# A mixture-of-experts layer behind linear attention: the router with its weights stationary, 32x32 transposes on VectorE, and residual sums with the second statistics ahead of the routing

## The reference

```python
Q, K, V = x @ wq.T, x @ wk.T, x @ wv.T                 # 64 wide
energy  = einsum('bnd,bne->bde', K, V)                 # over the 2048 tokens
out     = (Q @ energy * sqrt(3 / 64)) @ wo.T
```

```python
scores = sigmoid(x @ Wr)                               # 8 experts
idx    = top_k(scores + router_bias, 2)
w      = scores[idx] / (sum(scores[idx]) + 1e-9)       # cw: w at idx, 0 elsewhere
hid    = silu(x @ Wg[e]) * (x @ Wu[e])                 # e = 0..3, 128 wide
routed = sum_e cw[e] * (hid[e] @ Wd[e]) + (cw[4] + cw[6]) * x + cw[7] * relu(x)
out    = routed + causal_depthwise_conv(x, 4 taps) + conv_b
```

## Time and profile before

| | us |
|---|---|
| median of 3 timed runs (892.45 to 894.4) | 893.69 |
| the profiled execution | 893.6 |
| its span, from the first instruction to the last | 891.8 |

### The profile page before, as it was taken

One profiled execution on the slowest core, in us unless ns is written; L12 is line 12 of the kernel. 1 busy time (PEld: TensorE's weight loads), 2 busy tenths in 40 slices (PEclk: granted clock), 3 DMA queues, 4 the chain that ended last, 5 costly groups with the idle time before them and its releaser, 6 DMA issues.

```text
span 891.8 us, 16729 instructions
## 1 busy us (share of the span) xinstructions
PE 855.9 (96%) x5437; PEld 754.3 (85%) x5437; DVE 741.1 (83%) x2056; ACT 628.7 (71%) x1238; POOL 572.7 (64%) x654
## 2 busy tenths in 40 slices
PE   5789999999999999999999999999999999999997
PEld 4668989898888888988889888888888898788876
DVE  5758889988888998888898888899888887767775
ACT  5676777777687777778677777777777775655643
POOL 3336776667676657667666767666576766556663
PEclk9989999999999999999999999999999999999999
DMA  9111434543334543343544343454424344433333
GB/s 286 57 52 47 137 121 142 143 117 99 95 119 142 144 142 68 114 129 120 143 143 114 101 115 99 143 144 142 119 72 119 101 114 119 111 104 100 106 91 84
DMA packets 79446, 103.86 MB, mean 116 GB/s; under 512 B 6528, under 2 KB 58880, under 8 KB 79360
## 3 DMA queue, kind: packets, MB, share of 16 engines
q1 hardware_dynamic: 74752, 86.02, 30.4%
q0 software_dynamic: 4608, 16.78, 10.0%
HBM read 68.96 MB, written 17.04 MB: 96 GB/s over the span
## 4 chain that ended last, share of the span: by engine, by line
PE 66%; DVE 13%; POOL 12%; issue 5%; ACT 4%; DMA 0%; POOLq 0%; ACTq 0%; DVEq 0%
PE ps_gu L406 9%; PE ps_gu L408 9%; PE ps_gu L407 9%; POOL enx L1368 7%; PE ps_y L406 5%; PE ps_y L408 5%; PE ps_y L407 5%; PE ps_sh L543 4%; PE ps_sh L533 3%; POOL gate L1327 3%; PE ps_sh L516 2%; DVE stats L1065 2%; DVE acc L1057 2%; ACT x L840 2%; PE ps_y L456 2%
## 5 line engine op out<-in xcount | busy, mean ns | idle before, releaser
L1327 POOL TENSOR_TENSOR gate<-gate,cwb 128x512 f32<-128x512 f32 x128 | 167.5, 1309 | 127.8 <-ACT gate L763 126.4
L406 PE MATMUL ps_gu<-x2T_hi,wgu_hi 128*128 128x512 f32 x512 | 212.2, 414 | 0.0
L408 PE MATMUL ps_gu<-x2T_hi,wgu_lo 128*128 128x512 f32 x512 | 203.0, 396 | 0.0
L407 PE MATMUL ps_gu<-x2T_lo,wgu_hi 128*128 128x512 f32 x512 | 202.2, 395 | 0.0
L1368 POOL TENSOR_TENSOR enx<-inv_e,logits 128x32 f32<-128x32 f32 x32 | 177.5, 5546 | 8.6 <-ACT logits L756 8.6
L406 PE MATMUL ps_y<-wd_hi,hid_hi 128*128 128x256 f32 x512 | 152.8, 299 | 4.0 <-DVE hid_lo L1018 3.1
L1029 DVE SCALAR_TENSOR_TENSOR conv<-x2T,conv_w,conv 128x512 f32<-128x512 f32 x192 | 146.4, 801 | 0.0
L408 PE MATMUL ps_y<-wd_hi,hid_lo 128*128 128x256 f32 x512 | 145.3, 284 | 0.0
L407 PE MATMUL ps_y<-wd_lo,hid_hi 128*128 128x256 f32 x512 | 144.2, 282 | 0.0
L1011 DVE TENSOR_TENSOR hid<-ps_gu,gate 128x512 f32<-128x512 f32 x128 | 86.0, 672 | 39.2 <-POOL gate L1327 38.1
L408 PEld LDWEIGHTS ps_gu<-x2T_hi,wgu_lo 128*128 128x128 f32 x512 | 96.9, 189 | 22.5
(11 more groups left out here) (115 smaller groups left out, 1934.3 us busy)
## 6 DMA issues: line engine op xcount, KB each, us to landing
cwb<-cw_rows SPq DMA_DIRECT2D x128, 256.0 KB, 4.0
xa<-in_x SPq DMA_DIRECT2D x32, 512.0 KB, 7.5
acc<-in_x SPq DMA_DIRECT2D x32, 512.0 KB, 6.7
acc<-x POOLq DMA_DIRECT2D x32, 512.0 KB, 4.6
out<-acc SPq DMA_DIRECT2D x64, 256.0 KB, 2.3
cwb<-in_wg SPq DMA_DIRECT2D x4, 128.0 KB, 4.0
cwb<-in_wu SPq DMA_DIRECT2D x4, 128.0 KB, 3.8
cwb<-in_wd SPq DMA_DIRECT2D x1, 512.0 KB, 4.5
```

Source lines behind the costliest of these rows:

```text
L406: nc.tensor.matmul(dst, a_hi, b_hi, start=start, stop=False, skip_group_check=True)
L407: nc.tensor.matmul(dst, a_hi, b_lo, start=False, stop=False, skip_group_check=True)
L408: return nc.tensor.matmul(dst, a_lo, b_hi, start=False, stop=stop, skip_group_check=True)
L1327: g.tensor_tensor(gate[:, e % 2], gate[:, e % 2], cwb[:, q, e], ALU.mult).then_inc(gatew_ready, 1)
```

## The change

- **Router.** The stationary operand is now `wr2`: per half of the features 32 columns, of which 8 are the rounded `wr`, 8 its rest and 16 zero. Two matmuls run the rounded x2T past it and two the rest of x2T, each with 512 columns (all four tiles). The result is the transposed logits, 32 rows by 512.
- **Logits.** `logits_turn` on VectorE transposes them in 32x32 blocks out of PSUM and adds the high and the low half (`summed`, on 32 partitions). Four DMAs on SP (`move_logits`) lay them out on 128 partitions. ScalarE computes `size = |logits|`, `mag = size + 2**-100` and `dip = silu(-mag)`; VectorE makes the sigmoid of it, `minor = dip / mag`, `signed = (logits > 0) + minor`, `score = |signed|`. The power and `den` on GpSimd go.
- **Weights.** The 1e-9 is a ninth column of `raw`, so `wsum_eps` goes. A VectorE transpose in 32x32 blocks makes `cwT`, four DMAs store it. TensorE's `weights_transpose` and ScalarE's copy go.
- **Order.** `residual` and `norm2_stats` stand ahead of the routing in every step, which is in two halves (`route_scores`, `route_weights`); in `drain` steps `hid_low(2)` stands between them. `norm1_stats` moves behind `hidden(1)`, tap 1 ahead of the first `x2T_low`, tap 2 is split around the outputs. `halo` moves from VectorE to ScalarE. In `drain` steps `hid_high(2)` stands ahead of `silu(3)` and both ahead of `conv_begin`.
- **Head.** The first five transposes of xn use other banks and stand between Q, attention and Gram matrices in another order; attention of group 1 comes behind the first router; the first SiLU is asked for at once.

The core of the diff (the heads of ScalarE, VectorE and GpSimd are reordered to match):

```diff
+        wr2 = sb("wr2", [P, HC, SQ], F32R)
...
+            def move_logits(st):
+
+                sp.wait_ge(sum_ready, st.before("R", 1, 1))
+                if st.later("R", 1):
+                    sp.wait_ge(cw_ready, st.before("R"))
+                for j in range(P // SQ):
+                    sp.dma_start(logits[j * SQ:(j + 1) * SQ, :], summed[:, j].rearrange("p t e -> p (t e)"))\
+                        .then_inc(logits_loaded, 16)
+
             def spread_weights(st):
 
                 k = st.slot("R", 2)
                 rows = cw_rows[bass.ds(st.group("R"), 1)]
                 sp.wait_ge(cwT_ready, st.before("R", 1, 1))
-                sp.dma_start(rows.rearrange("a e (t n) -> (a e t) n", t=TG), cwT[:, :]).then_inc(cw_stored, 16)
-                sp.wait_ge(cw_stored, st.before("R", 16, 16))
+                for j in range(P // SQ):
+                    sp.dma_start(rows[:, :, :].rearrange("a e (t n) -> (a e t) n", t=TG)[:, j * SQ:(j + 1) * SQ],
+                                 cwT[j * SQ:j * SQ + EM * TG, :]).then_inc(cw_stored, 16)
+                sp.wait_ge(cw_stored, st.before("R", 64, 64))
...
+                    move_logits(st)
                     spread_weights(st)
...
             def router(st):
-                pe.wait_ge(x2T_ready, st.before("R", HC, HC))
+                if st.before("R") == 0:
+                    pe.wait_ge(wrlo_out, 1)
+                b, q = ps_sh[0][0:SQ, :], st.slot("R", 2)
                 pe.wait_ge(x2Tlo_ready, st.before("R", HC, 1))
-                b, q = ps_sh[0], st.slot("R", 2)
-                for t in range(TG):
-                    for c in range(HC):
-                        last = nc.tensor.matmul(b[:, t * NE:(t + 1) * NE],
-                                                x2T[:, q, c, PAD + t * P:PAD + (t + 1) * P], wr_sb[:, c],
-                                                start=(c == 0), stop=(c == HC - 1))
+                pe.wait_ge(x2Thi_ready, st.before("R", HC, HC))
+                for c in range(HC):
+                    nc.tensor.matmul(b, wr2[:, c], x2T_hi[:, q, c], start=(c == 0), stop=False,
+                                     skip_group_check=True)
+                for c in range(HC):
+                    if c == 1:
+                        pe.wait_ge(x2Tlo_ready, st.before("R", HC, HC))
+                    last = nc.tensor.matmul(b, wr2[:, c], x2T_lo[:, q, c], start=False, stop=(c == HC - 1),
+                                            skip_group_check=True)
                 last.then_inc(router_done, 1)
...
-                if st.before("B") == 0:
-                    pe.wait_ge(xnTlo_ready, 2 * HC - h)
-                elif st.before("B") == 1:
-                    pe.wait_ge(x1_ready, 1 + h)
-                elif h == 0:
+                if st.before("B") == 1:
+                    pe.wait_ge((x2Tlo_ready, turn_ready)[h], (HC, 1)[h])
+                elif st.before("B") > 1 and h == 0:
                     pe.wait_ge(x2Tlo_ready, st.before("R", HC, HC))
-                else:
-                    pe.wait_ge(logits_ready, st.before("R", 1, 1))
+                elif st.before("B") > 1:
+                    pe.wait_ge(turn_ready, st.before("R", 1, 1))
...
-            def weights_transpose(st):
-                pe.wait_ge(cw_ready, st.before("R", 1, 1))
-
-                if st.before("R") == 0:
-                    pe.wait_ge(xnTlo_ready, 5 * HC)
-                elif st.on("B"):
-                    pe.wait_ge(x1_ready, st.before("B", 2, 1))
-                else:
-                    pe.wait_ge(x2Tlo_ready, st.before("R", HC, HC))
-                nc.tensor.transpose(ps_sh[1][0:EM * TG, 0:P],
-                                    cw[:, st.slot("R", 2), 0:EM].rearrange("p e t -> p (e t)"), ident[:, :])\
-                    .then_inc(cwT_done, 1)
...
+                head_transpose(0)
                 pe.wait_ge(w_loaded, 16 * N_LOADS)
                 chain_gramT(b)
                 chain_p1(b)
                 chain_et(b)
+                q_project(at("Q", 0, NG))
                 pe.wait_ge(et_out, b.chains(2, 2))
                 chain_f(b)
+                attention(b, 0)
+                attention(b, 1)
+                head_transpose(1)
+                gram_matrix(at("A", 4, NG))
+                head_transpose(2)
                 q_project(at("Q", 1, NG))
-                for n in range(2):
-                    attention(at("B", n, NG), 0)
-                    attention(at("B", n, NG), 1)
-                gram_matrix(at("A", 4, NG))
-                r = at("R", 0, NG)
                 x2_transpose(r, 0)
                 x2_transpose(r, 1)
+                gram_matrix(at("A", 5, NG))
                 router(r)
-                xn_transpose(at("A", 2, NG), 0)
-                xn_transpose(at("A", 2, NG), 1)
-                xn_transpose(at("A", 3, NG), 0)
-                xn_transpose(at("A", 3, NG), 1)
+                attention(at("B", 1, NG), 0)
+                attention(at("B", 1, NG), 1)
...
-                if r_on:
-                    weights_transpose(st)
+                if b_on and drain:
+                    down(st, "C", 2)
                 if a_on and r_on:
                     xn_transpose(st, 0)
-                if c_on:
+                if c_on and not (b_on and drain):
...
-            def logits_copy(st):
-                act.wait_ge(router_done, st.before("R", 1, 1))
-
+            def halo(st):
+
+                q = st.slot("R", 2)
                 if st.later("R", 1):
-                    act.wait_ge(enx_ready, st.before("R"))
-                copy(logits[:, :], ps_sh[0][:, 0:TG * NE]).then_inc(logits_ready, 1)
+                    act.wait_ge(x2T_ready, st.before("R", HC))
+                if st.later("R", 2):
+                    act.wait_ge(conv_ready, st.before("R", CT, -CT))
+                if st.first("R"):
+                    copy(x2T[:, q, :, 0:PAD], ident[:, 0:HC * PAD].rearrange("p (c n) -> p c n", c=HC), 0.0)\
+                        .then_inc(halo_ready, 1)
+                else:
+                    copy(x2T[:, q, :, 0:PAD], x2T[:, 1 - q, :, GT:GT + PAD]).then_inc(halo_ready, 1)
+
+            def score_size(st):
+                act.wait_ge(logits_loaded, st.before("R", 64, 64))
+                if st.later("R", 1):
+                    act.wait_ge(cw_ready, st.before("R"))
+                nc.scalar.activation(size[:, :], logits[:, :], ACT.Abs).then_inc(size_ready, 1)
+                act.wait_ge(size_ready, st.before("R", 1, 1))
+                nc.scalar.activation(mag[:, :], size[:, :], ACT.Identity, bias=least[:, :]).then_inc(mag_ready, 1)
+
+            def score_dip(st):
+
+                act.wait_ge(mag_ready, st.before("R", 1, 1))
+                nc.scalar.activation(dip[:, :], mag[:, :], ACT.Silu, scale=-1.0).then_inc(dip_ready, 1)
...
+                if r_on:
+                    score_size(st)
+                    score_dip(st)
+                if c_on:
                     q = st.slot("C", 2)
                     act.wait_ge(skip_ready, st.before("C", 2, 2))
                     for t in range(TG):
@@ -966,15 +997,16 @@
                     for t in range(TG):
                         nc.scalar.activation(x2[:, q, t], x2[:, q, t], ACT.Relu, scale=cw[:, q, EM + 3, t:t + 1])\
                             .then_inc(relu_ready, 1)
+                if c_on and st.drain():
+                    hid_high(st, 2)
+                    silu(st, 3)
...
+                dve.wait_ge(mag_ready, st.before("R", 1, 1))
+                done(v.reciprocal(rmag[:, :], mag[:, :]))
+                dve.wait_ge(dip_ready, st.before("R", 1, 1))
+                after()
+                done(v.tensor_tensor(minor[:, :], dip[:, :], rmag[:, :], ALU.mult))
+                after()
+                done(v.scalar_tensor_tensor(signed[:, :], logits[:, :], 0.0, minor[:, :], ALU.is_gt, ALU.add))
+                after()
+                done(v.scalar_tensor_tensor(flat(score[:, :, :]), signed[:, :], -1.0, signed[:, :], ALU.mult, ALU.max))
...
+                dve.wait_ge(cw_ready, st.before("R", 1, 1))
+                if st.later("R", 1):
+                    dve.wait_ge(cw_stored, st.before("R", 64))
+                v.transpose(cwT[:, :], cw[:, q].rearrange("p e t -> p (e t)")).then_inc(cwT_ready, 1)
+
+            def logits_turn(st):
+                dve.wait_ge(router_done, st.before("R", 1, 1))
+                v.transpose(turned[:, :, :, :].rearrange("p j t n -> p t j n"),
+                            ps_sh[0][0:SQ, :].rearrange("p (t j n) -> p t j n", t=TG, j=P // SQ))\
+                    .then_inc(turn_ready, 1)
+                dve.wait_ge(turn_ready, st.before("R", 1, 1))
+                if st.later("R", 1):
+                    dve.wait_ge(logits_loaded, st.before("R", 64))
+                v.tensor_tensor(summed[:, :, :, :].rearrange("p j t e -> p (j t) e"),
+                                turned[:, :, :, 0:NE].rearrange("p j t e -> p (j t) e"),
```

(71 more changed lines are left out.)

261 lines of the change are left out of this document (133 added, 128 removed).

## The result

The changed kernel takes 932.14 us (median, 929.65 to 936.26) where the kernel before took 894.05 in the same session. The ratio is 1.041, with a 95% interval of 1.038 to 1.045: slower, where I had predicted 880 and faster. The profiled execution has a span of 931.0 us, before 891.8: 39.2 us to explain.

A forecast was written before the change was run, and what follows sets the result against it. TensorE was taken to set the pace, VectorE not far behind; after the change VectorE would make plain steps later. 893.6 + 8.6 (plain) - 6 (chain) - 5 (start) - 11 (end) = 880.2 us; range 854 to 901.

The forecast's parts named there:

- TensorE's part: Router and weights transpose on TensorE: 0.88 us less per step, a plain step 24.5 if nothing else bound it.
- VectorE's sum: VectorE's work from first x2T_lo to hid_lo(2): 17.6 us, making hid_lo(2) ready at 23.0 and a plain step 24.9.
- the collision with tap 2: Plain steps: tap 2's half waits 1.1 us on VectorE for GpSimd's second gate product; plain step 25.8.
- +8.6 us: The 19 plain steps together: 0.45 us more each than now.
- There is about 0.6 us of slack, which I cost at nothing: ScalarE waits for the logits DMAs until 14.7; 9 us of work behind fit before norm1's followers are wanted at 23.
- the second collision: Rival: small routing operations meet the fourth gate product, 1.1 us a step, 901 us; chance 0.18, shared with slow transpose.
- -6: Seven chain steps: TensorE has 3 us more work, hid_lo(2) is in time, so 0.88 us saved in each.
- -11: Last four steps, 768 to 866 us: no wait for cw, shorter router, 21.7 us each, 11 us gained.
- -5: Start: first pass of the loop 2 us earlier, its router 3 us cheaper; between 0 and -9.
- The reorder: VectorE: residual and norm2_stats ahead of the routing add 3.11 us before hid_lo(2); raw, no longer held, gives back 0.88.

The follow-up runs named there:

- late_turn: The version at 887 us with the turn and sum of the logits moved on VectorE from ahead of tap 2 to behind hidden(1): 873.3 us.
- before_reordered: Kernel before, with only residual sums and second statistics moved ahead of the routing in plain and chain steps: 889.0 us, ratio 0.992.
- tap_later: Changed kernel with the second half of tap 2 moved on VectorE from ahead of hidden(0) to behind hid_low(0): 920.1 us, ratio 1.026.
- old_taps_head: Changed kernel with VectorE's taps, first statistics and the work ahead of the steps back in the order of before: 929.4 us, ratio 1.038.
- late_gate3: before_reordered plus four idle 128x512 copies on ScalarE behind hid_high(1) in every step, without the new router: 919.0 us.
- early_silu3: old_taps_head with ScalarE's skip scaling and ReLU ahead of the sigmoid operations, silu(3) and hid_high(2) ahead of conv_begin: 901.9 us; same swap on the changed kernel: 904.7.
- low2_earlier: Changed kernel with hid_low(2) between route_scores and route_weights in every step, not only the last ones: 918.0 us, ratio 1.024.
- router_alone: Kernel before with the new router only, routing still ahead of residual sums and second statistics: 918.3 us, ratio 1.026.
- tap_and_low2: Changed kernel with the moves of both tap_later and low2_earlier: 910.8 us, ratio 1.016.
- the version at 887 us: early_silu3 with hid_low(2) between route_scores and route_weights, tap 1 ahead of x2T_low(0) and first statistics behind it: 887.2 us.

## Why the prediction was wrong

**TensorE's part** was right and worth nothing as it stood: 0.92 us for the router, the transpose gone, all hidden behind VectorE. It came through only in late_turn (24.88 per plain step against 25.11 in before_reordered), and 0.23 of 0.88 at that.

**VectorE's sum and the collision with tap 2.** Both stood. I had the tap at 7.7 us into the step, 1.1 us stretched, `hid_lo(2)` ready at 24.0, then 1.87 us to the next step. The trace has the tap at 484.15 - 476.48 = 7.67, `hid_lo(2)` ready at 500.51 + 0.65 - 476.48 = 24.68, and 503.09 - 501.22 = 1.87 behind. The difference of 0.68 is as large as what the stretched `two` costs (0.85 for 0.17), which my sum left out. It is not quite as clean as that: 8.8 + 14.6 + 0.7 is 24.1, and unrounded my plain step would have been 25.97 and the 19 of them +11.8 us, not +8.6. The turn took 0.69 (0.65 assumed), the sum 0.28 (0.3), the turn of `cw` 0.21 (0.22). My walk skipped `gate_up(4)`'s wait for `hidden(0)`, 0.94 us in the trace. It lies ahead of a later wait and probably costs nothing more, but no run shows that: in tap_later it is gone, and another wait has come in its place.

**The step that failed first: ScalarE's lateness, "There is about 0.6 us of slack, which I cost at nothing".** I had the wait for the logits and had the skip scaling behind it at 14.7 (measured 15.2). I asked whether ScalarE would be late for its own followers. The question to ask was what its lateness moves on GpSimd, and onto what that falls. It was in the text as a rival, the second collision, with the fourth product at 20.4 (measured 20.9), and it got only 0.18, a share of it for a slow transpose, because I asked whether one particular operation, `biased`, would be hit. The small operations stand in a row from `minor` at 496.5 to `cw` at 500.1, seven of them are held in one run or another, and a product of 1.3 us that falls into the row hits one nearly wherever it lands: in 17 steps of 26 here, in 26 of 26 in the kernel before, old_taps_head and late_gate3. Its price was sized 1.1 and measured 0.68 to 1.0. late_gate3 and the two early_silu3 show the cause from both sides: 27 to 30 us of the whole, less what the clock did in them. And with ScalarE's list put right the changed kernel's plain step takes 25.98 us, near the 25.8 of the forecast and at its unrounded 25.97. That it fits to the digit is luck: TensorE's wait for `hidden(0)` isn't in the sum.

**"-6" for the steps with the chain** failed on the sentence that hid_lo(2) is in time there. They grew by 0.95 us, and TensorE waits 1.2 to 1.4 us for hid_lo(2) in six of them and 3.2 in the last. ScalarE's copies of f stand ahead of `hid_high(0)`, VectorE loses 2.18 us there (2.36 before), and then has the same long list to `hid_low(2)`; moved ahead of the weights (low2_earlier), these steps fell to 27.97. I had added TensorE's extra work to its side and nothing to VectorE's.

**"-11" at the end** was off by 13.5. The walk had no wait of `norm2` for the ReLU, 2.8 us in three steps, and none of the ReLU for the logits. With ScalarE's list mended the stretch from step 34 takes 116.0, which is -7.7: most of the gain was there, and spent. Up to 3.5 us of that difference are the clock's, as said above.

**"-5" at the start** was off by 12. The first pass begins 0.9 us earlier, not 2, and step 7 loses 7.8: the routing stands ahead of `q_low(3)` on VectorE (3.76 us on TensorE), all taps stand ahead of `hidden(0)` (3.07), and up to 3.8 us are the clock's. With the new router and neither new order (router_alone) step 8 starts at 92.0, before at 88.2, in the changed kernel at 95.1, so about half of it seems to be the router's; the spread of that column is too large to say more.

The four misses add up: plain steps 14.6, chain 12.7, start 11.9, end 13.5, in sum 52.7, and 880.2 + 52.7 = 932.9. The rival with the second collision (1.1 us a step more, so 26.9 for a plain one) is the case that came true for the plain steps (26.60); its total, 901, is still 31 us short, for it left the other three terms as they were.

**The reorder.** My walk priced it at 3.11 us on VectorE ahead of `hid_low(2)`, less 0.88 for `raw`, and for the first round I expected +1.0 a step from it alone. It gained 0.27. The sum ahead of `hid_low(2)` is about right (3.11 - 0.88 = 2.2, measured 1.9 later), but there were 2 us of slack, and what the slack covers costs nothing. The gain came from TensorE's small wait for x2. Beside the new router, where the slack is spent, the same reorder costs 11 us (router_alone against old_taps_head): there my price was of the right kind.

## What to carry to other kernels

An engine with 6 us idle per step is not free to be late: ask which other engine its output starts, when that then runs, and which instructions of a third engine it falls on. Where a long operation of one engine holds up some of another's, put the instructions that don't mind (here those that read PSUM, and `bn_stats`) beside it, and look at the whole row of exposed ones, not at one of them. When a part is taken from the bound and the time rises, put the parts back one by one, and also in pairs: here one part gained by itself and lost beside the other. Look at the granted clock of each stretch before a difference of a few us is given a cause.

## What the runs showed of the hardware

- GpSimd's gate product (128x512, two SBUF inputs, 1.3 us) holds up some VectorE instructions until it ends and others not at all. Held in these traces: half taps (0.74 us, then up to 1.8), `hid_lo` (0.67, then 0.8 to 1.4), `signed`, `minor`, `raw` on 128x32 (0.19, then up to 1.2), and, which I had not expected, the copy of 128x8 with its single input (0.17, then 0.82 to 0.91, 13 times in the changed kernel's trace). Not held, in the changed kernel's trace: `bn_stats` (0.38 to 0.43 us, in 87 cases under a product as in 169 without), the maximum of eight, `match_replace`, `tensor_reduce`, the reciprocal, and all that read PSUM. The Trainium skill ("SBUF — State Buffer", SBUF: two separate sides) names an operation in a two-port mode beside one with two SBUF inputs; the copy agrees, and I had looked for two inputs only.
- GpSimd's power does not hold VectorE. In the kernel before, 61 `hid_lo` lay wholly under it and took at most 0.69 us, 48 half taps at most 0.75. By the same section of that page of the Trainium skill it would hold them as well; the trace does not show it.
- With GpSimd's small `coef` and `skip` operations of 128x4 it is the tap that holds them: in tap_and_low2 they took 0.20 us alone and mostly 0.59 to 0.71 beside a half tap, while 88 of 110 half taps beside them took their usual 0.74 and the other 22, which also touched a GpSimd `hid_lo`, up to 0.81.
- TensorE's granted clock was at half (1.2 GHz) for 14 to 24 us between 20 us and step 8 in every trace, and in some of them again later. In the changed kernel's step 7 it fell in a wait of 3.76 us and again 1 us behind one of 3.07. How long it is at half varies between kernels with the same instructions up to there: 13.7 us in before_reordered and 20.5 in late_gate3.
- VectorE's 32x32 transposes took 0.69 us for 32x512 out of PSUM, beside a gate product or not (0.69 to 0.71), and 0.21 us for 128x32 in SBUF.
- Matmuls of 32 stationary columns and 512 moving ones follow each other at the same 0.23 us as those of 128 columns.
- From the end of VectorE's turn of the weights to the first gate product lay 6.3 us (four stores, the wait for them, four loads) in old_taps_head (from 24.4 to 26.9 + 3.85 of a step). late_turn rules it out as the bound of the version at 887 us; what a shorter way would give was not tried.
